# A new instruction order and bank table for an attention and feed-forward pipeline, with two weight loads moved

## The reference, cut to what matters

```python
h = shift_token(x)
q, k, v = jnp.split(h @ wqkv, 3, axis=-1)          # 8 heads of 64
q = l2norm(q) * qs;  k = l2norm(k) * ksc
q, k = rotary_xpos(q, k)
o = local_attention(q, k, v)                       # windows of 128, each looks at itself and the one before
x = x + o @ wo
h = shift_token(x)
h = (h - mu) / jnp.sqrt(var + 1e-05) * lg + lb
a, g = jnp.split(h @ w1 + b1, 2, axis=-1)          # 682 hidden rows
x = x + (a * jax.nn.gelu(g, approximate=False)) @ w2 + b2
```

## Time and profile before

| | us |
|---|---|
| median of 3 runs | 4132.93 (4129.93 to 4137.37) |
| the profiled execution | 4137.37 |
| its span | 4135.6 |
| PE busy | 3954.6 (96%) |
| DVE busy | 3612.4 (87%) |
| ACT busy | 2746.1 (66%) |
| POOL busy | 2694.6 (65%) |

### The profile page before, as it was taken

The page is one execution under the profiler, slowest core; times in us unless marked ns, Lnnn a source line. Parts: engine busy times, 40 slices in busy tenths (PEclk is TensorE's granted clock), DMA queues, the critical chain, the costliest instruction groups (busy, mean ns, idle before and its releaser), DMA issues.

```text
span 4135.6 us, 61076 instructions
## 1 busy us (share of the span) xinstructions
PE 3954.6 (96%) x19870; PEld 2681.6 (65%) x19870; DVE 3612.4 (87%) x6114; ACT 2746.1 (66%) x5896; POOL 2694.6 (65%) x1298
## 2 busy tenths in 40 slices
...
DMA packets 119610, 295.11 MB, mean 71 GB/s; under 512 B 21288, under 2 KB 45664, under 8 KB 119296
## 3 DMA queue, kind: packets, MB, share of 16 engines
...
## 4 chain that ended last, share of the span: by engine, by line
PE 28%; DVE 16%; ACT 7%; issue 5%; POOL 1%; DVEq 0%; SPq 0%; DMA 0%; ACTq 0%; POOLq 0%
PE b_bank L1497 6%; PE b_bank L1348 6%; PE b_bank L1441 4%; PE b_bank L1427 3%; PE b_bank L1411 3%; ACT b_scores L1576 2%; PE b_bank L1400 2%; DVE b_scores L1810 2%; DVE b_qk_rot L1775 2%; PE b_bank L1476 2%; DVE b_qk L1759 2%; PE b_bank L1380 1%; DVE b_probs_t L1823 1%; DVE b_hn_part L1868 1%; ACT b_h_part L1649 1%
## 5 line engine op out<-in xcount | busy, mean ns | idle before, releaser
L824 POOL TENSOR_TENSOR a_state<-a_state,a_c_wide 128x1024 f32<-128x1024 f32 x512 | 1194.4, 2366 | 19.7 <-DVE a_state L766 19.7
L1706 POOL TENSOR_TENSOR b_scores<-b_scores,b_row_rate 128x1024 f32<-128x1024 f32 (+1 forms) x256 | 488.2, 1918 | 821.3 <-DVE b_row_rate L1827 821.3
L584 PE MATMUL a_y_sum<-a_state,a_ident 128*128 128x512 f32 x2048 | 951.4, 597 | 6.8 <-POOL a_state L824 6.8
L766 DVE TENSOR_TENSOR_SCAN a_state<-a_decay,a_slot 128x1024 f32<-128x1024 f32 x352 | 789.8, 2275 | 0.7
L584 PEld LDWEIGHTS a_y_sum<-a_state,a_ident 128*128 128x128 f32 x2048 | 387.3, 191 | 383.2 <-issue 316.7
L1348 PE MATMUL b_bank<-b_w_qkv,b_hx_part 128*128 128x512 f32 x2304 | 616.0, 408 | 18.6 <-DVE b_w_qkv L1922 8.5
L1679 POOL TENSOR_TENSOR b_by_cos<-b_qk,b_rotary 128x1024 f32<-128x1024 f32 x128 | 336.4, 2628 | 322.7 <-DVE b_qk L1759 320.6
L1576 ACT ACTIVATE b_scores<-b_scores,b_row_bias 128x256 f32<-128x256 f32 (+1 forms) x1024 | 480.4, 472 | 91.7 <-DVE b_row_bias L1816 91.6
L695 ACT ACTIVATE a_decay<-a_dt,a_neg_a 128x512 f32<-128x512 f32 x704 | 455.1, 712 | 114.3 <-DVE a_state L766 113.9
L1476 PE MATMUL b_bank<-b_hn_part,b_w 128*128 128x512 f32 x2112 | 512.6, 395 | 6.3 <-DVE b_hn_part L1730 6.2
L1348 PEld LDWEIGHTS b_bank<-b_w_qkv,b_hx_part 128*128 128x128 f32 x2304 | 422.9, 191 | 114.1 <-DVE b_probs_t L1823 9.9
...
## 6 DMA issues: line engine op xcount, KB each, us to landing
a_c_wide<-bc_rows SPq DMA_DIRECT2D x256, 512.0 KB, 3.8
...
```

Of the source, the lines that this page charges most:

```text
L584: last = nc.tensor.matmul(y_sum[dd][:], ident[:], state[state_ring.slot[q]][:, i, :], start=False, stop=(j == GROUPS - 1 and i == GROUP - 1))
L766: nc.vector.tensor_tensor_scan(flat(h), flat(factor), flat(term), 0.0, ALU.mult, ALU.add).then_inc(scan_done.sem, 1)
L824: nc.gpsimd.tensor_tensor(h[:], h[:], c_wide[c_ring.slot[q // 2]][:], ALU.mult).then_inc(cmul_done.sem, 1)
L1706: nc.gpsimd.tensor_tensor(probs, probs, row_rate[:, w, at].unsqueeze(2).to_broadcast([P, 4, hi - lo]), ALU.mult)\
```

## The change

`ORDER`, `BANK_OF` and `FIRST_ORDER` are replaced, and two loads are issued elsewhere. Line numbers of the changed kernel are two lower from `load_w_1`'s neighbourhood down to the end of the file (L1409 there is L1411 here), and one to five off inside SP's steps.

```diff
 ORDER = """
-onorm-:3 ptr-:3 att-:3 mask:0.0 mask:0.1 score:0.0 score:0.1 score:1.0 exp:0 psq:0 score:1.1 hxs:0 hxload:0 mask:1.0
...
+ptr-:3 v-:3 hxs:0 mask:1.0 vc-:3 mask:1.1 score:0.0 score:0.1 score:1.0 hxload:0 exp:0 rate:0 add:0 pss:0 score:1.1
...
+onorm:3 turn:1 turnc:0 turnc:1 ptc:3 mask+:0.0 mask+:0.1
 """
...
-            def load_qkv(i):
-
-                at = slice(i * INNER, (i + 1) * INNER)
-                for to, source in zip(w_qkv, parts_dram["qkv"]):
-                    sp.dma_start(to[:, :, at], source[:, :, at]).then_inc(qkv_loaded[i], 16)
+            def load_qkv():
+
+                for i, done in enumerate(qkv_loaded):
+                    at = slice(i * INNER, (i + 1) * INNER)
+                    for to, source in zip(w_qkv, parts_dram["qkv"]):
+                        sp.dma_start(to[:, :, at], source[:, :, at]).then_inc(done, 16)
...
             def load_hx(s, slot, layer, _):
-                if s < 3:
+                if s < 3 or s == BATCH:
                     sp.wait_ge(v_done.sem, v_done.at(s))
...
                 if s == BATCH:
                     for done, group in zip(moved, (early, late)):
                         sp.wait_ge(done, 3 * loads_of(group))
-                    sp.wait_ge(q_full.sem, q_full.at(s - 1, TILES))
-                    load_qkv(0)
-                    sp.wait_ge(k_full.sem, k_full.at(s - 1, TILES))
-                    load_qkv(1)
-                    sp.wait_ge(v_done.sem, v_done.at(s))
-                    load_qkv(2)
+                    load_qkv()
...
-                if s == BATCH + 2:
-                    sp.wait_ge(h2_done.sem, h2_done.at(BATCH))
-                    load_w_1()
-                    sp.wait_ge(x_out_done.sem, x_out_done.at(BATCH))
-                    for to, source in zip(w_2, parts_dram["w_2"]):
-                        sp.dma_start(to[:], source).then_inc(w_2_loaded, 16)
...
             def store(s, slot, layer, _):
+                if s == BATCH - 1:
+                    sp.wait_ge(h2_done.sem, h2_done.at(BATCH))
+                    for done, group in zip(moved, (early, late)):
+                        sp.wait_ge(done, 3 * loads_of(group))
+                    load_w_1()
                 sp.wait_ge(x_out_done.sem, x_out_done.at(s, CHUNKS))
                 sp.dma_start(stack_dram[s + BATCH], x_out[:]).then_inc(stored.sem, 16)
+                if s == BATCH - 1:
+                    for to, source in zip(w_2, parts_dram["w_2"]):
+                        sp.dma_start(to[:], source).then_inc(w_2_loaded, 16)
```

33 lines of the change are left out of this document (16 added, 17 removed).

## The result

The changed kernel takes 4182.81 us (median of 4 runs, 4180.55 to 4183.98), the kernel before 4135.15 beside it: the ratio is 1.0116, with a 95% interval of 1.0098 to 1.0134. I had forecast 4158.5. The direction was right, the size was not: 47.7 us slower instead of 25.6. The profiled execution spans 4184.4 us (before: 4135.6).

| stretch | before | after | difference |
|---|---|---|---|
| start to `hxs` of the third pass | 1891.2 | 1892.6 | +1.4 |
| 13 passes of layer 0, each | 70.80 | 71.66 | +11.1 |
| seam: three passes, from `hxs` of sequence 15 to that of sequence 18 | 212.8 | 227.3 | +14.5 |
| 13 passes of layer 1, each | 71.67 | 73.14 | +19.1 |
| last `hxs` to the end | 179.5 | 182.1 | +2.6 |

What follows compares the result with a forecast made beforehand. PE was taken as the bound. 30 full passes at +0.58 us gave +17.4, the seam +9, the fill 0, the drain -1: +25.4 us in all, so 4158.5 us on the median, range 4126 to 4187.

Steps and rivals of the forecast that it cites:

- Bound, and what can be lost: Full passes: PE is the bound; a new order changes only time inside the matmul stream, PE's waits and the seam.
- Crossings: One more entry into and exit from part-array matmuls on PE per pass: 0.15 + 0.19 = +0.34 us.
- `pt:2.1`: PE behind `ga:4`: new banks are free early, so the wait for the copy of `pt:2.0` goes, -0.34 us a pass.
- `mean`: PE behind `pt:0.1`: `mean` waits until ACT has copied `pt:0.0` out of its bank, +0.58 us a pass.
- Other waits … I count these at 0: Tight places at `pt:1.2`, `ga:0` and `ga:3` counted at 0; about 0.7 us a pass if each gave way.
- With 30 full passes that is +17.4 us: The sum of +0.58 us a full pass, applied to 30 full passes.
- The rows of sequence 18 … 0, above +2: Rows queued behind `w_2` land 1 to 2 us late, mostly covered before `pk:0`: 0, upper bound +2 us.
- Seam: Pass 15, ahead of `pk:0`: PE waits 6.7 us for late weights, then 2.4 at a lower clock; +9 us.
- Fill: First passes, paced by POOL's cuts and SP's stores: 0, with -10 to +10 us possible.
- Drain: Last passes: `turn` of sequence 30 fits where PE waited for `wo`, -1 us (-3 to +4).
- C: Rival: tight places mid-pass (`ga:0`, `pt:1.2`) give way, +1.2 us a pass, a 72 us pass, 4177 us; chance 0.22.

Runs made afterwards that it cites:

- e10: Kernel before the change, with score:2.1 moved behind mean:0 and v:1, adding one entry and one exit per pass; ratio to before 1.0044.
- e7: Kernel before the change, with one pair of banks exchanged: pt:2.1 in bank 3, pt:2.2 in bank 7; 4126.04 us, ratio to before 0.9977.
- e2: Changed kernel with mean in bank 0 instead of bank 3, all orders kept; ratio to before 1.0122.
- e3: Changed kernel with the store of layer 1's output tokens one pass later, behind the load of the next sequence's rows; ratio to before 1.0108.
- e1: Changed kernel with the loads at the seam put back as they were before the change; ratio to before 1.0105.
- e19: Changed kernel, mean and pt:1.2 in bank 0, half of group 1's normalising left out on GpSimd, VectorE's pt:1 copies on ScalarE; ratio to before 1.0054.

## Why the prediction was wrong in size

- Bound, and what can be lost: right. PE is the bound, with the same matmuls before and after.
- Crossings, +0.34: right in kind and nearly in size. e10 gives 0.34, with entry and exit the other way round (0.19 and 0.15, not 0.15 and 0.19), and the blocks of the changed kernel add up to 0.41.
- `pt:2.1`, -0.34: right (0.32 to 0.33 in the trace, 0.34 a pass in e7).
- `mean`, +0.58: the wait is there, 0.51. But it is no term of its own (e2).
- **"Other waits … I count these at 0"** is the step that failed within a pass. I had priced `mean` alone, and named `pt:1.2` for `pn:1` as within 0.1 us, and `sqs` and `var` as unchanged. `pt:1.2` adds 0.20, and the bank wait in `ga:3`, which I had also named, 0.12 (2.87 against 2.75 us over ten passes). `ga:0`, the third place I had named, doesn't wait (2.95 in both), and `var` with the block behind it costs 0.03 less than before. With 0.41, 0.51 and -0.32 for the terms above that makes 0.89 of the 0.94 us between 71.74 and 70.80. By the table a pass of layer 0 is 0.86 longer, not 0.58, over 29 full passes in both layers 8 us more. The waits I had down as separate prices, with 0.7 us if all gave way, are one shortfall of 0.84 us.
- Layer 1: "With 30 full passes that is +17.4 us" took a pass of layer 1 for one of layer 0, and this is the larger miss. I had walked the lists of PE, ScalarE and VectorE, not SP's, and so had nothing for the rows of the next sequence. In both kernels SP issues them behind the store of the tokens, at the end of a pass, and they land 4.3 to 6.5 us later. In the old order `hxs:0` came behind `score:1.1` and began 0.1 to 0.5 us behind the landing, so there was almost nothing to spare: in six of 13 passes it began 0.09 us behind it, as a step does that waits for its data; in the new order it is third in the pass. 0.63 us a pass, 8.2 us (e3).
- "The rows of sequence 18 … 0, above +2": PE waits 2.52 us for them where it waited for nothing before. The repairs take 2.1 to 2.4 of it, but it varies as much from kernel to kernel (1.01 in e2).
- Seam, +9 (6.7 and 2.4): right, 6.46 and 1.9 in the trace. Of the 10.2 us of e1, 8.0 are this term, the rest is the rows of sequence 18.
- Fill, 0: +1.4 up to the third `hxs`, in this pair. The kernel before was profiled at the high end of its kind, though: this point lies at 1884.8 to 1891.2 us in the five kernels built on the old order and at 1887.3 to 1896.9 in those on the new, 5 us later on average. So the term was probably not 0; the cause stays open. Drain, -1: +2.6. In e19 it is +1.0, so more than half of it seems to go with the waits within a pass; the cause of the rest was not tried.
- Rivals: C (72 us a pass, 4177) came nearest, and `pt:1.2` did give way as it says; it had 0.22. That its number is so near is luck: a pass of layer 0 is 71.66, not 72, and the late rows, which C doesn't have, make up the rest.

By the spans (48.8 against my 25.4) I was 23.4 us short: the late rows are 10 to 11 of it, the waits within a pass 8, drain, fill and seam the rest.
